# Decoder layer in FP32R pieces, cross-attention: one 128-column value stationary that holds high and low columns, the halves added by DVE and the context split by GpSimd

## The reference, cut to what matters

```python
# x: (32, 256, 256) after the first norm; ctx: (32, 120, 256); Wq, Wk, Wv: (256, 16, 64); Wo: (16, 64, 256)
q = einsum('bsd,dhk->bshk', x, Wq) * 64 ** -0.5
k = einsum('bsd,dhk->bshk', ctx, Wk)
v = einsum('bsd,dhk->bshk', ctx, Wv)
weights = softmax(einsum('bthk,bfhk->bhft', k, q), axis=-1)
out = einsum('bfhk,hkd->bfd', einsum('bhft,bthk->bfhk', weights, v), Wo)
```

## Time and profile before

| what | value |
|---|---|
| median of 3 runs | 3174.6 us (3172.29 to 3176.49) |
| span of the profiled execution, first to last instruction | 3171.4 us |
| outside the span, by the median | 3.2 us |
| mean granted TensorE clock of the profiled execution | 0.990 |
| TensorE matmuls busy | 3088.7 us, 97% of the span |
| DVE, ACT, GpSimd busy | 2256.1, 2142.4, 1581.9 us |

### The profile page before, as it was taken

How to read it: one execution, slowest core, us unless ns; L and a number is a source line. 1 busy time by engine, 2 the same in 40 slices (tenths; PEclk the granted TensorE clock), 3 DMA queues, 4 the chain that set the end, 5 groups by cost and what they waited for, 6 DMA issues and landing times. The chain is left out here.

```text
span 3171.4 us, 78666 instructions
## 1 busy us (share of the span) xinstructions
PE 3088.7 (97%) x22624; PEld 2900.2 (91%) x22624; DVE 2256.1 (71%) x6566; ACT 2142.4 (68%) x6930; POOL 1581.9 (50%) x2904
## 2 busy tenths in 40 slices
PE   6999999999999998999999999999989999999998
PEld 5999999999999987999999999999868888889998
DVE  6777777777877877778877778787745455544665
ACT  6888888888887877787877877777734444442222
POOL 3666766766676765333333333333446666653000
PEclk8999999999999999999999999999989999999999
DMA  6444444444444440121111111111245444533333
GB/s 181 117 120 125 127 125 121 121 120 122 127 111 111 125 143 24 48 64 45 54 55 45 57 55 44 64 45 48 94 118 119 100 98 101 128 56 85 120 124 106
DMA packets 193684, 300.70 MB, mean 95 GB/s; under 512 B 33856, under 2 KB 134080, under 8 KB 192704
## 3 DMA queue, kind: packets, MB, share of 16 engines
q1 hardware_dynamic: 168768, 262.91, 27.8%
q0 software_dynamic: 24576, 33.57, 6.2%
HBM read 116.02 MB, written 67.11 MB: 58 GB/s over the span
## 5 line engine op out<-in xcount | busy, mean ns | idle before, releaser
L964 POOL TENSOR_SCALAR ca_prob<-ca_prob,ca_inverse 128x120 f32<-128x120 f32 x1024 | 354.6, 365 | 632.5 <-DVE ca_inverse L1268 630.5
L665 ACT ACTIVATE sa_prob<-sa_prob,sa_shift 128x128 f32<-128x128 f32 (+1 forms) x1024 | 453.6, 461 | 2.6 <-DVE sa_shift L718 2.6
L1206 ACT ACTIVATE ca_prob<-bank,ca_shift 128x120 f32<-128x120 f32 x1024 | 353.7, 366 | 6.0 <-DVE ca_shift L1262 3.5
L460 POOL TENSOR_SCALAR sa_prob<-sa_prob,sa_inverse 128x128 f32<-128x128 f32 x512 | 198.5, 388 | 234.5 <-DVE sa_inverse L726 220.4
L718 DVE CUSTOM_DVE_ANT_0 sa_prob<-bank,sa_mask 128x128 f32<-128x128 f32 (+1 forms) x1024 | 304.7, 352 | 6.9 <-PE bank L138 2.7
L136 PE MATMUL bank<-sa_ow,sa_y_hi 128*128 128x256 f32 x1024 | 279.6, 304 | 0.0
L136 PE MATMUL bank<-sa_kvT_a,sa_q 128*128 128x128 f32 (+1 forms) x1024 | 251.7, 281 | 17.7 <-DMA sa_q<-sa_q_tile 17.4
L138 PE MATMUL bank<-sa_kvT_b,sa_q 112*128 112x128 f32 (+1 forms) x1024 | 261.6, 281 | 0.0
L749 DVE TENSOR_TENSOR sa_pT_lo<-bank,sa_pT_hi 128x384 fp32r<-128x384 f32 x512 | 258.3, 544 | 1.8 <-ACT sa_pT_hi L650 1.8
L138 PE MATMUL bank<-sa_ow,sa_y_lo 112*128 112x256 f32 x1024 | 258.8, 283 | 0.0
L462 POOL TENSOR_SCALAR sa_prob<-sa_prob,sa_inverse 128x256 f32<-128x256 f32 x512 | 244.9, 478 | 0.0
(11 more groups left out here) (259 smaller groups left out, 12014.1 us busy)
## 6 DMA issues: line engine op xcount, KB each, us to landing
sa_q<-sa_q_tile SPq DMA_DIRECT2D x128, 288.0 KB
sa_q<-sa_q_tile SPq DMA_DIRECT2D x160, 112.0 KB
mid_x2T<-ca_x2T SPq DMA_DIRECT2D x32, 512.0 KB, 3.0
ex_sx<-mid_x2T SPq DMA_DIRECT2D x32, 512.0 KB, 3.3
sa_q<-sa_q_tile SPq DMA_DIRECT2D x304, 32.0 KB, 3.0
sa_xT_raw<-in_xT SPq DMA_DIRECT2D x32, 256.0 KB, 2.8
sa_q<-sa_q_tile SPq DMA_DIRECT2D x32, 256.0 KB
sa_x_res<-in_x SPq DMA_DIRECT2D x32, 256.0 KB, 2.8
```

Of the source, the lines that this page charges most:

```text
L460: pool.tensor_scalar(prob[:, r, hh, 0:P], prob[:, r, hh, 0:P], inverse[:, r, 2 * hh:2 * hh + 1], 1.0, ALU.mult, ALU.mult)
L665: act.activation(prob[:, r, hh, cols], prob[:, r, hh, cols], ACT.Exp, bias=shift[:, r, n:n + 1], scale=-1.0, accum_out=total[:, r, n:n + 1 ...
L964: ins = pool.tensor_scalar(prob[:, r, t, hh], prob[:, r, t, hh], inverse[:, r, n:n + 1], 1.0, ALU.mult, ALU.mult)
L1206: act.activation(prob[:, r, t, hh], SC[g % 2][:, n * S:n * S + S], ACT.Exp, bias=shift[:, r, n:n + 1], accum_out=total[:, r, n:n + 1]).the ...
```

## The change

The values of a pair of heads become one tile `v` of [120, 2, 8, 2, 128]. For the first head its 128 columns are `[high | low]`, for the second `[low | high]`. Two matrix products a head, with the high and the low part of the weights as the moving tile, give a [128, 256] result of which the head's own 64 rows hold the high values' product and the other 64 rows the low values' product; the low-by-low term, left out before, comes in too. The two heads write to two halves of the CX bank. ACT copies the "other" rows of each half to SBUF, onto the head's own rows (`c_other`), DVE adds them to the own rows of the bank into a new tile `c`, and GpSimd splits `c` into `c_hi` and `c_lo`, at the head of its slot g + CL + 1, ahead of the softmax scalings. The next CX now waits for the add (`csum_done`). The two fills with zeros of the gaps in `v_hi` and `v_lo` go, and with them TensorE's wait for them.

```diff
-    v_hi, v_lo = al.split("v", [S, 2, NP, 3 * DH])
+    v = al.sb("v", [S, 2, NP, 2, 2 * DH], F32R)
+    c, c_other = al.sb("c", [P, RING, T]), al.sb("c_other", [P, 2, T])
...
-            zeros = [k_hi[0:DH, :, :, S:2 * S], ..., v_hi[:, :, :, DH:2 * DH], v_lo[:, :, :, DH:2 * DH]]
+            zeros = [k_hi[0:DH, :, :, S:2 * S], ...]
...
# GpSimd
+            g = m - CL - 1
+            if step_exists(J, g):
+                r = g % RING
+                need(pool, o_mm, upto(J, g - RING))
+                need_alone(pool, csum_done, upto(J, g), spare_pool)
+                pool.tensor_scalar(c_hi[:, r], c[:, r], 1.0, 1.0, ALU.mult, ALU.mult).then_inc(cxhi_done, 1)
+                need_alone(pool, cxhi_done, upto(J, g), spare_pool)
+                pool.tensor_tensor(c_lo[:, r], c[:, r], f32(c_hi[:, r]), ALU.subtract).then_inc(cxlo_done, 1)
...
# TensorE
-                need(pe, cxlo_done, upto(J, g - 1))
+                need(pe, csum_done, upto(J, g - 1))
                 for hh in range(2):
-                    win = slice(hh * DH, hh * DH + 2 * DH)
-                    mm = three(pe, CX[:, 0:T], v_hi[:, b, p, win], v_lo[:, b, p, win], pT_hi[:, r, hh], pT_lo[:, r, hh],
-                               hh == 0, hh == 1)
+                    both = CX[:, hh * T:(hh + 1) * T]
+                    pe.matmul(both, v[:, b, p, hh], pT_hi[:, r, hh], start=True, stop=False, skip_group_check=True)
+                    mm = pe.matmul(both, v[:, b, p, hh], pT_lo[:, r, hh], start=False, stop=True, skip_group_check=True)
...
# ACT, values (DVE's subtraction goes to the other 64 columns likewise)
-                    ins = act.activation(v_hi[:, b % 2, n * NP // 2:(n + 1) * NP // 2, hh * 2 * DH:hh * 2 * DH + DH],
+                    ins = act.activation(v[:, b % 2, n * NP // 2:(n + 1) * NP // 2, hh, hh * DH:hh * DH + DH],
...
# ACT, context
-                need(act, o_mm, upto(J, g - RING))
-                act.activation(c_hi[:, r], CX[:, 0:T], ACT.Copy).then_inc(cxhi_done, 1)
+                need(act, csum_done, upto(J, g - 2))
+                for hh in range(2):
+                    own, other = slice(hh * DH, hh * DH + DH), slice((1 - hh) * DH, (2 - hh) * DH)
+                    ins = act.activation(c_other[own, g % 2], CX[other, hh * T:(hh + 1) * T], ACT.Copy)
+                ins.then_inc(other_done, 1)
...
# DVE, context
-                need(dve, cxhi_done, upto(J, g))
-                dve.tensor_tensor(c_lo[:, r], CX[:, 0:T], f32(c_hi[:, r]), ALU.subtract).then_inc(cxlo_done, 1)
+                need(dve, other_done, upto(J, g))
+                need(dve, cxlo_done, upto(J, g - RING))
+                for hh in range(2):
+                    own = slice(hh * DH, hh * DH + DH)
+                    ins = dve.tensor_tensor(c[own, r], CX[own, hh * T:(hh + 1) * T], c_other[own, g % 2], ALU.add)
+                ins.then_inc(csum_done, 1)
```

More of the change, by code:

```diff
@@ L853, in cross_attention @@
     chi_done, clo_done = al.sem("chi_done"), al.sem("clo_done")
+    other_done, csum_done = al.sem("other_done"), al.sem("csum_done")
     x_tr, xThi_done, xTlo_done = al.sem("x_tr"), al.sem("xThi_done"), al.sem("xTlo_done")
@@ L938, in first_values @@
             pool.memset(half[:], -0.5).then_inc(const, 1)
-            zeros = [k_hi[0:DH, :, :, S:2 * S], k_lo[0:DH, :, :, S:2 * S], k_hi[DH:P, :, :, 0:S], k_lo[DH:P, :, :, 0:S],
-                     v_hi[:, :, :, DH:2 * DH], v_lo[:, :, :, DH:2 * DH]]
+            zeros = [k_hi[0:DH, :, :, S:2 * S], k_lo[0:DH, :, :, S:2 * S], k_hi[DH:P, :, :, 0:S], k_lo[DH:P, :, :, 0:S]]
             for n, t in enumerate(zeros):
@@ L943, in first_values @@
                 pool.memset(f32(t), 0.0).then_inc(const, 1)
-            pool.wait_ge(const, 7)
+            pool.wait_ge(const, 5)
             for q in range(SEQS):
@@ L988, in tensor @@
     def tensor(pe):
-        first_use = {1: (cross.w_lo, KC), QL: (cross.w_lo, KC * (len(CROSS) - 1)), SL: (const, 5), QL + 1: (cross.o_read, B), CL: (const, 7),
+        first_use = {1: (cross.w_lo, KC), QL: (cross.w_lo, KC * (len(CROSS) - 1)), SL: (const, 5), QL + 1: (cross.o_read, B),
                      OL: (cross.w_lo, KC * (len(CROSS) - 1) + 1), GATE: (gate_done, 1)}
@@ L1247, in slot @@
                 for hh in range(2):
-                    at = (slice(None), b % 2, slice(n * NP // 2, (n + 1) * NP // 2), slice(hh * 2 * DH, hh * 2 * DH + DH))
-                    ins = dve.tensor_tensor(v_lo[at], v_bank(J, b, n)[0:S, :].rearrange("s (p h k) -> s p h k", h=2, k=DH)[:, :, hh],
-                                            f32(v_hi[at]), ALU.subtract)
+                    of = v[:, b % 2, n * NP // 2:(n + 1) * NP // 2, hh]
+                    ins = dve.tensor_tensor(of[:, :, (1 - hh) * DH:(2 - hh) * DH],
+                                            v_bank(J, b, n)[0:S, :].rearrange("s (p h k) -> s p h k", h=2, k=DH)[:, :, hh],
+                                            f32(of[:, :, hh * DH:hh * DH + DH]), ALU.subtract)
                 ins.then_inc(vlo_done, 1)
```

## The result

The changed kernel takes 3206.05 us (median of 4 runs, 3205.18 to 3207.9) against 3174.63 us for the kernel before on the same chip: 31.4 us slower, ratio 1.0097 with a 95% interval of 1.0085 to 1.0109. I had said 3149. The profiled execution's span is 3206.2 us.

The account below looks back on a forecast made before the run. TensorE, busy 97% of the span, was taken as the bound. Of 7.5 us saved a body 4.3 are given back; 3171.4 - 8 x 3.3 + 1.5, with 3.2 outside the span, gave 3149 us, range 3120 to 3175.

Parts of the forecast that it names:

- TensorE, removed: Context product: six 256-column matmuls become four a step, saving 7.5 us a body, 60 us in all, as the gain's ceiling.
- DVE, changed: Context on DVE: one 128x256 subtraction becomes two 64x256 additions, 0.87 us between starts, 0.53 us more a step.
- What DVE does to the gain: Cross-attention loop: with DVE and TensorE full in different slots, 4.3 of the 7.5 us a body are given back.
- My walk: Following TensorE and DVE through the 32 slots of a body; it gave 132.9 us before the change, only differences used.
- the walk's three places: Slots 2-4 and 18-20 (2.1 us a body), 10-12 and 26-28 (1.2), and the body's end, paid in slots 0 and 24 (1.0).
- ACT, costed at nothing: Context copy on ACT: two 64x256 copies add 0.50 us a step, costed at nothing because the value slots cover it.
- The cover: Value slots, where TensorE has 1.4 us more, absorb ACT's extra; without them some 0.3 us in 4 slots of 32.
- GpSimd, costed at nothing in the loop: Split of the context on GpSimd, ahead of its scalings: 1.22 us a step, with a slot as cover, costed at nothing.
- GpSimd comes late: Rival, chance 0.05: two 0.74 us operations queued before the scalings make short slots late, costing 20 to 30 us; 3170 to 3180.
- one rival that makes the kernel slower: DVE becomes the bound in short slots 10 to 15 and 26 to 31, 10 us longer, 3185; chance 0.10.
- Ends of the stage: Removed fills give nothing; in the drain the context's longer chain loses 1.5 us, between 0 and 4.
- The rule beside it: Port lock: DVE's norm multiply would wait for GpSimd's subtraction, up to 0.74 us in 16 slots, 12 us against, time 3161.

Follow-up runs that it names:

- e11: Changed kernel with all added work left out: one 128-row copy on ACT, one 128-row addition on DVE, no split on GpSimd; 3127.2 us.
- e13: Changed kernel with one 128-row copy on ACT and no split on GpSimd, so only DVE's pair of additions is left; 3158.3 us.
- e14: Changed kernel with one 128-row addition on DVE and no split on GpSimd, so only ACT's pair of copies is left; 3140.4 us.
- e8: Changed kernel without GpSimd's split: DVE's pair writes the high part, which the output products also take as the low part; 3168.9 us.
- e12: e10 with DVE's residual add placed ahead of the low part of v in its slot; 3183.9 us.
- e10: Changed kernel with GpSimd's split placed after its softmax scalings, and the last nine steps split by ACT and DVE; 3191.6 us.
- e7: Changed kernel with one 128-row addition on DVE and one 128-row copy on ACT, so only GpSimd's split is left of the added work; 3152.3 us.
- e9: Changed kernel with the split of the last nine steps made by ACT (high part) and DVE (low part) in place of GpSimd; 3196.5 us.
- e6: Changed kernel with one 128-row copy on ACT in place of the pair, DVE's pair and GpSimd's split kept; 3193.4 us.
- e2: Kernel before the change, with DVE's subtraction for the context's low part made in two halves of 64 rows; 3200.9 us.

## Why the prediction was wrong, step by step

**TensorE, removed: right.** 7.5 us a body was the ceiling, and e11 comes to 128.29 from 134.57, 6.3.

**DVE, changed: right.** I took 0.87 us from the pair's start to the next, and it is 0.89 (DVE's timeline after, slots 2 and 3):

```profile
1751.36 0.42 DVE L1288 TENSOR_TENSOR ca_q_lo<-bank,ca_q_hi 128x256 fp32r<-128x256 f32 x1 [0.28 <-ACT ca_k_hi L1181]
...
1752.55 0.86 DVE L1302 TENSOR_TENSOR ca_c<-bank,ca_c_other 64x256 f32<-64x256 f32 x2
1753.44 0.69 DVE L1308 TENSOR_TENSOR ca_pT_lo<-bank,ca_pT_hi 120x512 fp32r<-120x512 f32 x1
...
1755.95 0.39 DVE L1288 TENSOR_TENSOR ca_q_lo<-bank,ca_q_hi 128x256 fp32r<-128x256 f32 x1
```

From q's low part to the next are 4.59 us, where I said 4.55. It answers to the earlier trace rows.

**What DVE does to the gain: mechanism right, size short.** With DVE's pair alone the body is 132.58, 5.5 us above the 127.05 that 7.5 us less would be; I said 4.3. Of the 5.5, 1.2 are missing in e11 already, where DVE has nothing added; the pair itself adds 4.3. My walk had 0.9 (the 0.47 of slots 2 and 3 that could not be had, twice) and 3.4 for the two. The distance between neighbouring starts of ACT's high part of q, by slot and as the mean of the six bodies, tells where: e13 is longer than e11 by 0.55 us in slot 3 and in 19, by 0.67 in slots 11 and 12 together and in 27 and 28, by 0.26 in slot 24 and by 1.28 in slots 31 and 0. These are the walk's three places, with 0.6, 0.6, 0.3 and 0.7 there; 0.3 in slots 15 and 16 it did not have. So the term that was too small is the end of the body. The walk had a slot begin after TensorE or after q's low part, and nothing else, but there the value product also waits for the low part of the transposed context (3.7 us in e13, 0.65 a body); no run tells how much of the 1.28 that makes.

**ACT, costed at nothing: wrong.** The cover was to be the value slots, and 0.3 us in 4 slots without it. ACT's pair adds 1.0 us to the body alone (e14), 1.5 beside DVE's pair (e13 to e8). In e14 TensorE's one large wait is for the residual add, 1.3 us a body. That add is DVE's, and it stands in DVE's queue behind the low part of v, which waits for ACT's high part: ACT's delay comes out on another engine, in an instruction that the change doesn't touch (the rows at 1716.59 and 1717.26 above show the order and the wait in the kernel after). Of e14's 1.0 us, 0.5 lie in slot 10 and 0.5 in slot 26, where that add is; the other slots cancel. e12, where the add stands ahead of v, has lost that wait and 7.7 us against e10. So the value slots, which I named as ACT's cover, are where its delay is paid, since DVE's whole queue hangs on it there.

**GpSimd, costed at nothing in the loop: wrong, and the largest error of the loop.** The durations were right: 0.41 and 0.74 us against my 0.48 and 0.74. Groups by line after, 1300 to 2200 us:

```profile
L965 POOL TENSOR_TENSOR ca_c_lo<-ca_c,ca_c_hi 128x256 fp32r<-128x256 f32 x211 | 155.4, 737 | 38.7 <-POOL ca_c_hi L963 38.7
...
L963 POOL TENSOR_SCALAR ca_c_hi<-ca_c 128x256 fp32r<-128x256 f32 x210 | 86.1, 410 | 75.5 <-issue 75.0 <-DVE ca_c L1302 0.5
```

I had written that the split "waits for the add of the slot before, which is over about 2 us before the reciprocal". That holds in the slot that loses as well: the sum is over at 1719.67 and the reciprocal at 1722.29. What failed is that I took this add for the only thing that holds the split. Ahead of it in the queue stands the norm's small operation, which waits for DVE's statistics until 1721.73 and is through at 1722.41, after the reciprocal. From there the split (1.31 us with 0.18 between its two halves) is paid in front of the scalings, and these end last. By the distances between ACT's high parts of q, e7 is longer than e11 by 0.98 us in slot 12 and again in slot 28, and by less than 0.1 in any other: that is the whole of the 2.0 us a body that the split costs alone. Beside both pairs it costs 2.7, of which these two slots have 2.0. GpSimd was idle for 1.54 us just before, with the sum there, so it is the order as much as the amount that costs; no run puts the split ahead of the norm's operation. My small rival "GpSimd comes late" had the short slots and the queue ahead of the scalings right and, at 20 to 30 us against the 25 of e7, the price. Its condition, two operations of 0.74 us each, did not hold, so the price was in part luck. It had 0.05. The chances also did not fit each other: slower had 0.09 in all, and one rival that makes the kernel slower 0.10.

**Ends of the stage: wrong by nearly ten times.** I had 1.5 us, at most 4, for the drain; it is 13.0 after step 255. I counted the latency of the new chain and not what stood ahead in GpSimd's queue; e8, without the split, takes 11.4 us less after step 255, and e9 gets 9 of them back by taking the last splits out of the queue. The 7.3 us of the last 15 steps come for the most part where the split and DVE's pair are both there: steps 240 to 255 take 66.7 us in the kernel after and 65.2 in e6, but 60.3 in e8, 59.6 in e13 and 58.0 in e7 (62.1 in e14, 59.5 before). The wait of 3.6 us for the scaled weights lies in them, in the slots with a search round. The scalings wait there for DVE's reciprocal, which comes after the round. That chain I read from the timelines; no run takes it apart. Behind the wait TensorE's matmuls start 0.21 us apart until 2296.3, in place of 0.12, which by an estimate from these distances is some 2 to 3 us more.

The sum, in bodies: 127.05 for TensorE, 5.5 for DVE's pair, 1.5 for ACT's, 2.7 for the split, 136.8; I had 127.0 + 4.3 + 0 + 0. Eight bodies of 5.5 us too little are 44, the last steps and the drain some 13 net (what is left of the 57; the first bodies lose less than the rest), and these 57 are what parts 3149 from 3206.

**The rule beside it.** The norm's multiply has the median that it had before, now at L1315 (64 of them: shortest, median, longest), against the earlier trace rows:

```profile
L1315 DVE TENSOR_SCALAR ca_x<-ca_res,ca_meanvar,ca_rstd x64: 404/407/499, 1283.1 to 2336.5; 128x256 f32<-128x256 f32 x64
```

In 15 of the 64 it began 0.1 us after GpSimd's high part of c and took 0.49 to 0.50 us, and that instruction 0.44 to 0.46 in place of 0.41. GpSimd's subtraction falls on it once in the whole stage, for 0.07 us. In the other slots with a norm the scalings fall beside it: four of them take 1.58 to 1.60 us there and 1.40 elsewhere. In the kernel before that happened once (1.57 against 1.39, at 2280.98); in 15 other places the multiply took 0.56 to 0.58 us beside scalings that kept their time. One of the places is GpSimd's slot 27, the row at 1723.72 above, where these 0.18 us are in TensorE's wait. By the Trainium skill, SBUF — State Buffer, section Who interferes with whom, the one that comes second blocks for the whole of the other's instruction; the row shows 0.18 us over four scalings, less than half of one multiply. No run here shows the 12 us that the rule would have given.

**What stays open.** Why DVE is idle for 2.9 us at the start of a body in e2 alone; what the split would cost ahead of the norm's operation; what makes the 10 us of interplay between DVE's pair and the split (in the profiled executions 13, of which 10 fall after step 240); and the 3.3 us wait in the last search slots that e10 still has.

## What to carry to other kernels

An average busy share of 35% on a third engine does not price work given to it: walk its queue through the fullest slot, with everything that stands ahead of the new instructions, what that waits for, and everything behind them, and do the same for the drain, where the queue holds the next stage's loads and gathers. When a change takes from the engine that is full and adds to three that feed it, price the additions each by a kernel with that one alone; here 48 us were won and 79 given away, in pieces of 13, 31, 25 and 10. An instruction on half of the rows cost as much here as a whole one (0.42 us for each half on DVE, 0.42 for the whole before), so a layout that needs two halves doubles that step on every engine that it passes.

## What the runs showed of the hardware

DVE was idle for 0.3 us ahead of its first instruction of a body before, 0.6 after and 2.9 in e2, with the same loop and one instruction more in each slot. Two dependent GpSimd instructions, the second waiting on the first's semaphore, stand 0.18 us apart, on the mean of 211. And a TensorE stall near the end of a stage costs more than its length: behind waits of 3.6, 2.9 and 4.5 us the granted clock was 0.64 to 0.85 over 54 us, with matmuls 0.21 us apart at the 1.2 GHz level in place of 0.12. Waits of up to 1.15 us in the loop left it at 1.00 (the window of one body).
